# Fourth edge stage of a four-layer graph network: two of every 56 tiles gathered by SyncE and ScalarE

## The chip, the core and the metric

The kernel runs on one core of one Trainium2 chip. The core has a matrix engine (TensorE, PE in the profile), a vector engine (VectorE, DVE), an activation engine (ScalarE, ACT), a general engine (GpSimd, POOL) and a sequencer without arithmetic that issues DMAs (SyncE, SP), all of which run side by side and wait for each other on semaphores. Sixteen DMA engines move data between HBM and the on-chip memory. The metric is the device time of one execution in microseconds (us), the median of several.

## What is computed

Four graph layers run one after the other on 6250 nodes of 128 channels and the same 206250 edges, which are sorted by their target `dst`. Each layer normalises the nodes, gathers a row for each edge's source, and sums the rows per target. The fourth, the only one that the change touches, is the plainest:

```
def _L3_gnn_ref(x, edge_index, W, bias, ln_gamma, ln_beta):
    h = x @ W
    ...                      # src, dst: the edges and one loop per node
    deg = segment_sum(ones, dst)
    dinv = where(deg > 0, rsqrt(deg), 0)
    norm = dinv[src] * dinv[dst]
    agg = segment_sum(h[src] * norm[:, None], dst) + bias
    y = relu(layernorm(agg) * ln_gamma + ln_beta)
    return y + x
```

## The kernel before

The edges are cut into tiles of P = 128, four tiles (U = 4) to a group; 403 groups (EDGE_GROUPS), so 1612 tiles, hold all of them. Before the fourth edge stage the kernel has written `table3` to HBM: one row of 128 floats (512 bytes) per node, `h` times `dinv` of the source. The edge stage then does, for each tile, three things. GpSimd gathers the 128 rows of the tile's sources from `table3` with one indirect DMA (L1623), which takes the 128 node numbers from a column of `index`. VectorE makes, for a whole group at once, the matrices `hot` of zeros and ones (L189, in `one_hots`) that say which edge belongs to which of 128 consecutive targets. TensorE multiplies the rows by `hot` (L1681; every float32 product is two passes of the array, so 3224 matrix instructions) into `psS`, and VectorE adds the result to the window of `ACC` that begins at the tile's first target (L1656). The window's address comes from a register that VectorE's sequencer loads (L196, in `windows`).

The program of this stage is written out group by group, not as a loop, and the order on each engine is the order of the code. Four row buffers (R = 4) hold the rows of four groups. GpSimd may gather into a buffer when VectorE has done all additions of the group four before and has counted `s_done` up (L1620, L1658). TensorE waits for `hot` of its group, for the four tiles of rows, and for a free quarter of `psS`. VectorE makes `hot` one group ahead and then adds tile by tile. At the stage's start VectorE clears `ACC` (L1644) before it gives GpSimd its first four counts (L1645). SyncE loads `index` and three rows of parameters (L1610, L1612), and has nothing more to do until the stage is over; ScalarE scales 98 node tiles (L1632, L1636) and then has nothing more to do either. Once the last addition is done, a barrier of all engines (L1607) leads into the closing node stage.

Three other places are read below because they show what SyncE's and ScalarE's DMA instructions take. In the first edge stage SyncE issues, for each batch of 32 tiles, 32 DMAs whose source row is in a register (L632, 128 partitions each), after one register load for every four of them (L196), and between batches DMAs at fixed addresses (L641, L642), while ScalarE issues 512 KB loads (L679). In the second edge stage it issues windows (L1085, 128 partitions) and lengths (L1094, 8 partitions), both with the source row in a register. The program's first stage has loads at fixed addresses.

## Time and profile before

| | |
|---|---|
| median of 3 runs | 9777.23 us (9772.35 to 9777.35) |
| profiled execution, its own time | 9774.57 us |
| its span, first to last instruction | 9772.8 us |
| fourth edge stage, first gather to last addition | 7691.6 to 9709.3 us |
| share of the span: GpSimd, VectorE, TensorE, ScalarE | 74%, 65%, 54%, 18% |

The profile is of one execution. PE is TensorE's matrix work, PEld its weight loads, DVE VectorE, ACT ScalarE, POOL GpSimd, SP SyncE; a q behind an engine marks its sequencer. Lines are those of the kernel before. "issue" is time in which an engine waited for nothing that the profile shows. The shares over the whole span mix stages with different limits, so the change has to be read in the last fifth of the span, where its stage lies.

### The profile page before, as it was taken

The numbers are of one execution on the slowest core, as the hardware profiler recorded it, in microseconds if no ns is written. First come the engines' busy times: TensorE is split into PE (matmuls) and PEld (weight loads), VectorE is DVE, ScalarE is ACT, GpSimd is POOL, SyncE is SP. The second block draws the span as 40 slices with busy tenths as digits, with TensorE's granted clock in tenths as the row PEclk, the third lists the DMA queues.
The fourth block names the chain that finished last, engine by engine and source line by source line (L and its number), as shares of the span: only waits on it lengthen the run. The fifth ranks groups of instructions, "written<-read, shape, count | busy, mean of one in ns | idle before, by whom it ended". The sixth has DMA issues, their size and how long they took to land. (4 is left out here: it accounts for less than half of the span.)

```text
span 9772.8 us, 131915 instructions
## 1 busy us (share of the span) xinstructions
PE 5246.3 (54%) x29478; PEld 4593.4 (47%) x29478; DVE 6386.1 (65%) x17574; ACT 1742.3 (18%) x3229; POOL 7215.7 (74%) x6460
## 2 busy tenths in 40 slices
PE   2334333345555555555555488888888544444443
PEld 1333333334445444555555377777777433333333
DVE  4667766676777776666666588888888533333334
ACT  2222222221222222111111111111111200000001
POOL 3777777771888888888888477777777577777775
PEclk5555555556555555555555699999999655555555
DMA  5555554442776667777777422222222222222221
GB/s 137 130 121 125 125 129 112 117 116 63 111 111 109 109 110 112 113 109 108 109 110 112 101 56 56 56 57 57 57 56 56 54 53 53 53 53 53 53 53 52
DMA packets 1095241, 861.72 MB, mean 88 GB/s; under 512 B 408856, under 2 KB 931359, under 8 KB 1094342
## 3 DMA queue, kind: packets, MB, share of 16 engines
q0 software_dynamic: 386880, 427.12, 25.5%
q1 hardware_dynamic: 677460, 320.18, 14.4%
q10 hardware_dynamic: 30436, 109.19, 3.4%
q8 instruction: 174, 2.85, 0.1%
q14 instruction: 291, 2.38, 0.1%
HBM read 706.10 MB, written 149.64 MB: 88 GB/s over the span
## 5 line engine op out<-in xcount | busy, mean ns | idle before, releaser
L1286 POOL DMA_INDIRECT sums<-sumrows,index x1612 | 2521.8, 1564 | 674.5 <-issue 312.9
L670 POOL DMA_INDIRECT rows<-table,index x1612 | 1612.5, 1000 | 629.3 <-issue 485.6
L1623 POOL DMA_INDIRECT rows<-table,index x1612 | 1522.0, 944 | 570.5 <-issue 490.6
L1427 POOL DMA_INDIRECT rows<-table,index x1612 | 1547.7, 960 | 513.1 <-issue 393.7
L1681 PE MATMUL psS<-hot,rows 128*128 128x128 f32 x3224 | 824.7, 437 | 1207.4 <-issue 1142.4
L1681 PEld LDWEIGHTS psS<-hot,rows 128*128 128x128 f32 x3224 | 717.7, 328 | 1314.4 <-issue 1266.6
L1254 PE MATMUL psX<-same,hotW 128*128 128x128 f32 x3224 | 811.9, 431 | 970.3 <-DVE hotW L1157 970.0
L1656 DVE TENSOR_TENSOR ACC<-ACC,psS 128x128 f32 x1612 | 465.3, 289 | 1201.4 <-PE psS L1681 1087.9
L1254 PEld LDWEIGHTS psX<-same,hotW 128*128 128x128 f32 x3224 | 702.0, 320 | 1095.7 <-DVE hotW L1157 1095.1
L1263 PE MATMUL psV<-win,mix 128*128 128x129 f32 x3224 | 800.9, 425 | 346.4 <-ACT mix L1220 341.3
L1518 PEld LDWEIGHTS psS<-hot,mid 128*128 128x128 f32 x6448 | 869.9, 196 | 38.9 <-issue 5.7
L1263 PEld LDWEIGHTS psV<-win,mix 128*128 128x128 f32 x3224 | 686.7, 314 | 397.5 <-issue 397.5
L1518 PE MATMUL psS<-hot,mid 128*128 128x128 f32 x6448 | 868.8, 279 | 5.4 <-DVE mid L1484 4.0
L1454 DVE TENSOR_TENSOR ACC<-ACC,psS 128x256 f32 x1612 | 660.1, 410 | 17.3 <-PE psS L1518 12.7
L820 DVE TENSOR_TENSOR ACC<-ACC,psA 128x128 f32 x1612 | 465.5, 289 | 273.1 <-issue 65.8
L1174 DVE CAST index<-place 128x4 int32<-128x4 f32 x403 | 76.4, 189 | 782.1 <-DMA sums<-sumrows,index 781.7
L1503 PE MATMUL psA<-base,w 16*128 16x256 f32 x806 | 271.3, 416 | 368.5 <-issue 355.5
L1157 DVE TENSOR_SCALAR hotW<-K,REL,weight 128x128 f32<-128x128 f32 x1612 | 462.1, 371 | 0.0
L1224 ACT COPY sumrows<-psV 128x516 f32<-128x516 f32 x403 | 237.4, 589 | 1097.7 <-PE psV L1263 619.1
L1220 ACT COPY mix<-psX 128x512 f32<-128x512 f32 x403 | 236.2, 586 | 1101.6 <-PE psD L1257 1012.2
L1511 PE MATMUL psW<-w,h 128*128 128x128 f32 x3224 | 430.9, 277 | 1.1 <-ACT h L1439 1.1
L1437 ACT ACTIVATE h<-psA,b 128x256 f32<-128x256 f32 x403 | 191.1, 474 | 1169.8 <-PE psA L1503 1169.8
(303 smaller groups left out, 9559.0 us busy)
## 6 DMA issues: line engine op xcount, KB each, us to landing
win<-table SPq DMA_DIRECT2D x1612, 64.5 KB
srow<-src_f SPq DMA_DIRECT2D x403, 256.0 KB, 4.2
rows<-table,index POOLq DMA_INDIRECT x4836, 2.5
HN<-rel_f ACTq DMA_DIRECT2D x102, 512.0 KB, 4.4
relB<-rel_f ACTq DMA_DIRECT2D x102, 512.0 KB, 4.3
er<-limbs SPq DMA_DIRECT2D x1632, 3.0 KB
sums<-sumrows,index POOLq DMA_INDIRECT x1612
ACC<-edge_marks SPq DMA_DIRECT2D x204, 96.0 KB
```

The lines of the kernel that those rows point to most:

```text
L670: nc.gpsimd.indirect_dma_start(out=rows[:, r, k, :], out_offset=None, in_=table0[:, :], in_offset=bass.IndirectOffsetOnAxis(ap=index[:, n ...
L820: nc.vector.tensor_tensor(own, own, psA[:, j % 4, u * P:(u + 1) * P], ALU.add).then_inc(s_free, 1)
L1157: last = nc.vector.tensor_scalar(hotW[:, s, u, :], lane, REL[:, bass.ds(n * U + u, 1)], weight[:, bass.ds(n * U + u, 1)], ALU.is_equal, AL ...
L1254: last = nc.tensor.matmul(psX[:, u, :], hotW[:, s, u, :], same[:, s, u, :], start=True, stop=True)
L1263: last = nc.tensor.matmul(psV[:, s, u, 0:W1], mix[:, s, u, :], win[:, r, u, :], start=True, stop=True)
L1286: nc.gpsimd.indirect_dma_start(out=sums1[u][:, :], in_=sums[:, s, u, :], in_offset=None, compute_op=ALU.add, out_offset=bass.IndirectOffse ...
L1427: nc.gpsimd.indirect_dma_start(out=rows[:, n % R, u, :], out_offset=None, in_=table2[:, :], in_offset=bass.IndirectOffsetOnAxis(ap=index[: ...
L1454: nc.vector.tensor_tensor(own, own, psS[:, u, :, 0:P], ALU.add).then_inc(s_free, 1)
L1518: done = nc.tensor.matmul(psS[:, u, b, 0:P], mid[:, r % 2, u, b * C:(b + 1) * C], hot[:, r % 2, u, :], start=True, stop=True)
L1623: nc.gpsimd.indirect_dma_start(out=rows[:, n % R, u, :], out_offset=None, in_=table3[:, :], in_offset=bass.IndirectOffsetOnAxis(ap=index[: ...
L1656: nc.vector.tensor_tensor(own, own, psS[:, u, 0:P], ALU.add).then_inc(s_free, 1)
L1681: nc.tensor.matmul(psS[:, u, 0:P], rows[:, r, u, :], hot[:, r % 2, u, :], start=True, stop=True).then_inc(s_sum, 1)
```

## The change

SyncE and ScalarE each take one tile of every 14 groups off GpSimd. In groups 6, 20, 34, ... (29 of them) it is SyncE that gathers the fourth tile, in groups 13, 27, 41, ... (28 of them) ScalarE; GpSimd gathers only three tiles in these groups. A tile taken over is gathered row by row: the helper loads its 128 node numbers from HBM as one row of integers, loads them four at a time into registers, and issues one DMA of one row (512 bytes, into one partition) for each. So a tile costs its helper 32 register loads and 128 DMAs. The rows go into two buffers of the helper's own, used in turn; the node numbers are fetched one tile ahead.

The number of row buffers goes from 4 to 8 and of `hot` buffers from 2 to 3, and `psS` holds four whole groups instead of four tiles. GpSimd waits for TensorE's products of the group eight before (`s_sum`) instead of VectorE's additions of the group four before, and no longer waits for the clearing of `ACC`. VectorE makes `hot` of group n and then adds the results of group n - 2, and it waits for all four products of that group before the first of its additions. TensorE waits in a helper's group for the helper's 128 rows ahead of the fourth product.

```diff
-        gathered2, gathered3 = pool_sems("gathered2_", 4), pool_sems("gathered3_", 4)
+        gathered2, gathered3 = pool_sems("gathered2_", 4), pool_sems("gathered3_", 8)
...
-                R = 4
...
+                R = 8
+                RS = 3
                 index = sb("index3", [P, T], I32)
                 rows = sb("rows3", [P, R, U, C])
-                hot = sb("hot3", [P, 2, U, P])
-                psS = ps("psS3", [P, 4, 512])
+                hot = sb("hot3", [P, RS, U, P])
+                EVERY = 14
+                firsts_of = (("sp", 6), ("act", 13))
+                extra = {key: sb("rows3" + key, [P, 2, C]) for key, _ in firsts_of}
+                numbered = {key: sb("index3" + key, [1, 2, P], I32) for key, _ in firsts_of}
+                s_number = {key: sem("s_number_e3" + key, 2) for key, _ in firsts_of}
+                s_extra = {key: sem("s_extra_e3" + key, 2) for key, _ in firsts_of}
+                def helper(n):
+                    for key, at in firsts_of:
+                        if n % EVERY == at:
+                            return key
+                    return None
+                def tiles_of(n):
+                    return U if helper(n) is None else U - 1
+                def gathered_by(n):
+                    return sum(tiles_of(m) for m in range(n % R, n + 1, R))
...
+                def own_gather(eng, key, at):
...
+                    groups = list(range(at, EDGE_GROUPS, EVERY))
+                    def numbers_of(j):
+                        eng.dma_start(numbered[key][:, j % 2, :], a["src_rows"][groups[j] * U + U - 1:groups[j] * U + U, :]).then_inc(s_number[key][j % 2], 16)
+                    numbers_of(0)
+                    for j, n in enumerate(groups):
+                        if j + 1 < len(groups):
+                            numbers_of(j + 1)
+                        if j > 1:
+                            eng.wait_ge(s_sum, (groups[j - 2] + 1) * U)
+                        eng.wait_ge(s_number[key][j % 2], 16 * (j // 2) + 16)
+                        for p in range(0, P, U):
+                            _, sources = nc.values_load_multi_w_load_instructions(
+                                numbered[key][0:1, j % 2, p:p + U], engines=(eng.engine,), min_val=0, max_val=N - 1,
+                                skip_runtime_bounds_check_because="a src is a node number")
+                            for k in range(U):
+                                eng.dma_start(extra[key][p + k:p + k + 1, j % 2, :], table3[bass.ds(sources[k], 1), :]).then_inc(s_extra[key][j % 2], 16)
+                    for r in range(2):
+                        eng.wait_ge(s_extra[key][r], 16 * P * uses(len(groups), 2, r))
...
+                        own_gather(sp, *firsts_of[0])
...
                         for n in range(EDGE_GROUPS):
-                            pool.wait_ge(s_done, n + 1)
+                            if n >= R:
+                                pool.wait_ge(s_sum, (n - R + 1) * U)
                             pool.nop(nofuse=True)
-                            for u in range(U):
+                            for u in range(tiles_of(n)):
...
+                        own_gather(act, *firsts_of[1])
...
-                        dve.sem_inc(s_done, R)
-                        dve.sem_inc(s_free, 4)
-                        one_hots(hot[:, 0, :, :], 0, numbers).then_inc(s_hot, 1)
-
-                        def add(n, g, r):
-                            if not (isinstance(n, int) and n == last):
-                                one_hots(hot[:, (r + 1) % 2, :, :], n + 1, numbers).then_inc(s_hot, 1)
+                        def adds(n):
                             firsts = windows(dve, n * U)
                             for u in range(U):
-                                dve.wait_ge(s_sum, n * U + (u + 1))
-                                own = ACC[:, 0, bass.ds(firsts[u], P)]
-                                nc.vector.tensor_tensor(own, own, psS[:, u, 0:P], ALU.add).then_inc(s_free, 1)
-                                dve.wait_ge(s_free, n * U + (u + 5))
-                            dve.sem_inc(s_done, 1)
-
-                        dve.wait_ge(s_rowsB, 48)
-                        for g in range(TN // TG):
-                            for r in range(R):
-                                add(R * g + r, g, r)
-                                at = slice(g * TG, (g + 1) * TG)
-                                if r == 1:
-                                    dve.wait_ge(s_own, g + 1)
-                                    nc.vector.tensor_tensor(own[:, at, :], own[:, at, :], rowsB[:, 0, :].unsqueeze(1).to_broadcast([P, TG, C]), ALU.add)
-                                if r == 3:
-                                    dve.wait_ge(s_gate, g + 1)
-                                    nc.vector.tensor_tensor(X[:, at, :], X[:, at, :], hn[:, at, :], ALU.add)
-                        for n in range(R * (TN // TG), EDGE_GROUPS):
-                            add(n, n // R, n % R)
+                                dve.wait_ge(s_sum, (n + 1) * U)
+                                if n * U + u > 0:
+                                    dve.wait_ge(s_free, n * U + u)
+                                total = ACC[:, 0, bass.ds(firsts[u], P)]
+                                nc.vector.tensor_tensor(total, total, psS[:, n % 4, u, :], ALU.add).then_inc(s_free, 1)
+                        for n in range(EDGE_GROUPS):
+                            one_hots(hot[:, n % RS, :, :], n, numbers).then_inc(s_hot, 1)
+                            if n > 1:
+                                adds(n - 2)
...
+                        adds(EDGE_GROUPS - 2)
+                        adds(EDGE_GROUPS - 1)
...
-                        def sums(n, g, r):
+                        for n in range(EDGE_GROUPS):
                             pe.wait_ge(s_hot, n + 1)
-                            pe.wait_ge(s_rows[r], 16 * U * g + 16 * U)
+                            pe.wait_ge(s_rows[n % R], 16 * gathered_by(n))
+                            if n >= 4:
+                                pe.wait_ge(s_free, (n - 3) * U)
                             for u in range(U):
-                                pe.wait_ge(s_free, n * U + (u + 1))
-                                nc.tensor.matmul(psS[:, u, 0:P], rows[:, r, u, :], hot[:, r % 2, u, :], start=True, stop=True).then_inc(s_sum, 1)
-
-                        straight(EDGE_GROUPS, R, sums)
+                                own = rows[:, n % R, u, :]
+                                if u >= tiles_of(n):
+                                    key, j = helper(n), n // EVERY
+                                    pe.wait_ge(s_extra[key][j % 2], 16 * P * (j // 2 + 1))
+                                    own = extra[key][:, j % 2, :]
+                                nc.tensor.matmul(psS[:, n % 4, u, :], own, hot[:, n % RS, u, :], start=True, stop=True).then_inc(s_sum, 1)
```

GpSimd, in the fourth edge stage (rows: a tile's gather is one row, merged with its count).

```order
 L140 UNCONDITIONAL_BRANCH
-L1615 UNCONDITIONAL_BRANCH
-L1623 DMA rows<-table,index 128x128 x1612
-L1607 UNCONDITIONAL_BRANCH
+L1658 UNCONDITIONAL_BRANCH
+L1667 DMA rows<-table,index 128x128 x1555
+L1649 UNCONDITIONAL_BRANCH
```

GpSimd has 57 gathers fewer; its order is otherwise the same.

SyncE, at the start of the same stage: `index3sp` holds node numbers, `rows3sp` is SyncE's own buffer of rows, ISA is the register arithmetic ahead of a DMA.

```order
+L1654 DMA rowsB<-in_L_gnn_ln_beta 128x128
+L1624 DMA index3sp<-in_src_rows 1x128 x2
+L1634 TENSOR_LOAD index3sp [waits s_index_e03]
+L1638 ISA
+L1638 DMA rows3sp<-table 1x128
+L1638 ISA
+L1638 DMA rows3sp<-table 1x128
+L1638 ISA
+L1638 DMA rows3sp<-table 1x128
+L1638 ISA
+L1638 DMA rows3sp<-table 1x128
+L1634 TENSOR_LOAD index3sp
```

Where SyncE had nothing behind its fourth load, the pattern of one register load and four row DMAs stands 32 times for each of 29 tiles. ScalarE gets the same behind its 98 activations, for 28 tiles.

VectorE, the first additions of the stage, before:

```order
L1644 MEMSET ACC 128x6400
L189 TENSOR_TENSOR hot<-psK,REL 128x512 x2
L196 TENSOR_LOAD D
L1656 ISA
L1656 TENSOR_TENSOR ACC<-ACC,psS 128x128
L1656 ISA
```

and with the change:

```order
L1689 MEMSET ACC 128x6400
L189 TENSOR_TENSOR hot<-psK,REL 128x512 x2
L1710 TENSOR_TENSOR own<-own,rowsB 128x896
L189 TENSOR_TENSOR hot<-psK,REL 128x512
L196 TENSOR_LOAD D
L1698 ISA
L1698 TENSOR_TENSOR ACC<-ACC,psS 128x128
L1698 ISA
```

A third `hot` now stands ahead of the first addition, and the additions of a group stand one group further back; the number of instructions is the same.

## Rows read from the trace of the kernel before

**Rows 1.** Busy time by stretch: length, PE, PEld, DVE, ACT, POOL, TensorE clock, DMA share, GB/s.

```profile
1000.00:1400.00 400.00, 151.07 (x1012) 137.52 (x1012) 276.19 (x722) 90.76 (x94) 306.64 (x306) 0.59 0.54 127
8000.00:9000.00 1000.00, 409.47 (x1601) 356.18 (x1600) 370.17 (x1003) 0.00 (x0) 755.94 (x802) 0.50 0.20 53
```

**Rows 2.** Timeline in mid-stage: start, length, engine, line, operation, [idle before <-releaser].

```profile
8501.17 0.94 POOL L1623 DMA_INDIRECT rows<-table,index  x1 [0.30 <-issue]
...
8502.49 2.04 PE L1681 MATMUL psS<-hot,rows 128*128 128x128 f32 x8 [2.88 <-issue]
8503.39 0.29 DVE L1656 TENSOR_TENSOR ACC<-ACC,psS 128x128 f32 x1 [2.45 <-PE psS L1681]
...
8503.88 1.14 DVE L1656 TENSOR_TENSOR ACC<-ACC,psS 128x128 f32 x3 [0.21 <-PE psS L1681]
...
8505.17 0.69 DVE L189 TENSOR_TENSOR hot<-psK,REL 128x512 f32<-128x512 f32 x1
```

**Rows 3.** GpSimd's gathers of the fourth stage: ns min/median/max, first and last start.

```profile
L1623 POOL DMA_INDIRECT rows<-table,index x1612: 940/944/1187, 7691.6 to 9703.5; - x180
```

**Rows 4.** Waits from 7700 to 9700 us: total us, times, longest us.

```profile
POOL rows L1623 <- issue: 488.1, 1602, 0.3
```

**Rows 5.** GpSimd's gathers from 490 to 2200 us: busy us, mean ns, idle before.

```profile
L670 POOL DMA_INDIRECT rows<-table,index x1310 | 1312.4, 1002 | 399.3 <-issue 394.1 <-PE psA L851 5.2
```

**Rows 6.** Timeline at the fourth stage's start, one row of each engine.

```profile
7685.07 0.43 SPq L1612 DMA_DIRECT2D rowsB<-in_L_gnn_ln_beta  x1
...
7685.40 5.39 DVE L1644 MEMSET ACC<- 128x6400 f32 x1 [1.32 <-issue]
...
7691.62 0.94 POOL L1623 DMA_INDIRECT rows<-table,index  x1 [79.62 <-DVEq L1645]
...
7698.08 14.40 ACT L1636 ACTIVATE HN<-HN,RSTD 128x128 f32<-128x128 f32 x49
```

**Rows 7.** DMA issues of the page: count, KB each, median us to landing.

```profile
index<-in_src_cols SPq DMA_DIRECT2D x2, 816.0 KB, 4.5
...
index<-in_src_batches SPq DMA_DIRECT2D x51, 16.0 KB, 2.3
```

**Rows 8.** Timeline at the fourth stage's end.

```profile
9703.54 0.94 POOL L1623 DMA_INDIRECT rows<-table,index  x1 [0.30 <-issue]
...
9706.71 2.04 PE L1681 MATMUL psS<-hot,rows 128*128 128x128 f32 x8 [3.56 <-issue]
...
9708.11 1.14 DVE L1656 TENSOR_TENSOR ACC<-ACC,psS 128x128 f32 x3 [0.21 <-PE psS L1681]
```

**Rows 9.** Sequencers' DMA and register-load instructions by line: ns min/median/max, starts.

```profile
L632 SPq DMA_DIRECT2D er<-limbs x1632: 332/333/24072, 97.2 to 2159.7; - x182
...
L1094 SPq DMA_DIRECT2D radius<-in_weight_rows x808: 276/277/349, 2410.5 to 5395.0; - x162
...
L641 SPq DMA_DIRECT2D ACC<-edge_marks x204: 302/421/1583, 151.5 to 2176.6; - x102
...
L642 SPq DMA_DIRECT2D rowm<-tile_marks x51: 298/310/336, 153.4 to 2177.1; - x51
...
L429 ACTq DMA_DIRECT2D ends_i<-in_dst_last x1: 328/328/328, 6.0 to 6.0; - x1
...
L196 DVEq TENSOR_LOAD <-D x1209: 337/343/604, 196.0 to 9703.8; - x173
L196 SPq TENSOR_LOAD <-D x811: 293/301/1444, 95.5 to 5401.8; - x163
```

**Rows 10.** Timeline of SyncE's issues: start, us from first start to last end, count.

```profile
1011.24 19.47 SPq L632 DMA_DIRECT2D er<-limbs  x32
...
1012.82 1.17 SPq L632 DMA_DIRECT2D er<-limbs  x2
...
1014.18 0.85 SPq L632 DMA_DIRECT2D er<-limbs  x2
...
3001.09 2.15 SPq L1094 DMA_DIRECT2D radius<-in_weight_rows  x5
```

More of the change, by code:

```diff
@@ L1594, in build @@
                 sb, ps, sem = alloc(st)
-                R = 4
-                last = EDGE_GROUPS - 1
+                R = 8
+                RS = 3
                 index = sb("index3", [P, T], I32)
                 rows = sb("rows3", [P, R, U, C])
-                hot = sb("hot3", [P, 2, U, P])
-                psS = ps("psS3", [P, 4, 512])
+                hot = sb("hot3", [P, RS, U, P])
+                EVERY = 14
+                firsts_of = (("sp", 6), ("act", 13))
+                extra = {key: sb("rows3" + key, [P, 2, C]) for key, _ in firsts_of}
@@ L1601, in build @@
+                psS = ps("psS3", [P, 4, U, P])
                 numbers = ps("psK3", [P, 512])[:, 0:P]
-                s_chain, s_hot, s_sum, s_free, s_done = (sem(n + "_e3") for n in ("s_chain", "s_hot", "s_sum", "s_free", "s_done"))
+                s_chain, s_hot, s_sum, s_free = (sem(n + "_e3") for n in ("s_chain", "s_hot", "s_sum", "s_free"))
                 s_rows = gathered3
@@ L1626, in _ @@
                         for r in range(R):
-                            pool.wait_ge(s_rows[r], 16 * U * uses(EDGE_GROUPS, R, r))
+                            pool.wait_ge(s_rows[r], 16 * gathered_by(EDGE_GROUPS - 1 - (EDGE_GROUPS - 1 - r) % R))
                     @block.scalar
@@ new lines, in _ @@
+                        for n in range(EDGE_GROUPS):
+                            one_hots(hot[:, n % RS, :, :], n, numbers).then_inc(s_hot, 1)
+                            if n > 1:
+                                adds(n - 2)
+                            g, r = divmod(n, 4)
+                            at = slice(g * TG, (g + 1) * TG)
+                            if n == 0:
+                                dve.wait_ge(s_rowsB, 48)
+                            if g < TN // TG and r == 1:
+                                dve.wait_ge(s_own, g + 1)
+                                nc.vector.tensor_tensor(own[:, at, :], own[:, at, :], rowsB[:, 0, :].unsqueeze(1).to_broadcast([P, TG, C]), ALU.add)
+                            if g < TN // TG and r == 3:
+                                dve.wait_ge(s_gate, g + 1)
+                                nc.vector.tensor_tensor(X[:, at, :], X[:, at, :], hn[:, at, :], ALU.add)
```

## The prediction, made before the changed kernel had run

> **What bounds the kernel now.** I read the busy time by stretch first, because the shares of the whole span mix the stages. From 8000 to 9000 us, the inside of the fourth edge stage, GpSimd is busy 756 of 1000 us and no other engine over 410; ScalarE does nothing and the DMA engines are 20% busy [rows 1]. The timeline shows the pattern: gathers of 0.94 us, each after 0.30 us of idle time that waits for nothing [rows 2], 1602 such gaps, 488 us, and practically no wait for another engine [rows 4]. So GpSimd issues without a pause, and a tile costs (9703.5 - 7691.6) / 1611 = 1.249 us [rows 3]. A group's four tiles take 5.0 us. VectorE works on a group for 0.69 us of `hot` and four additions, each (1.14 - 0.29) / 2 = 0.43 us after the one before, 2.4 us together, and waits for TensorE's products; TensorE works for 2.04 us and idles 2.9 [rows 2]. TensorE's granted clock is 0.50, the 1.2 GHz level, all through [rows 1], and nothing in this sum needs the other. The stage's time is the number of GpSimd's gathers times 1.249 us, and a start and an end.
>
> **What GpSimd sheds.** SyncE takes 29 tiles and ScalarE 28, so 57 of 1612 gathers go: 57 x 1.249 = 71.2 us, all on the path, if the helpers keep up. At the start GpSimd no longer waits for the clearing of `ACC`, which ends at 7690.8, 0.8 us ahead of the first gather [rows 6]. What is late next is the index: issued some 1.3 us ahead of the last row of parameters, so at 7683.7 to 7684.1, and 4.5 us to landing [rows 6, 7], 7688.6. With the same 0.8 us the first gather starts at 7689.4, 2.2 us earlier. At the end VectorE now waits for all four products of the last group. Before, its last addition ended at 9709.25, 5.7 us after the last gather began; now it has four additions, 4 x 0.43, behind the last product, about 1.9 us after TensorE's start at 9706.7: 9710.3, so 1.0 us more [rows 8]. Net: 71.2 + 2.2 - 1.0 = 72.4 us, and the stage would end at 9636.9.
>
> **What it costs elsewhere if the helpers keep up.** VectorE has the same instructions in another order, under a cover of 5.0 - 2.4 = 2.6 us a group. TensorE has the same products. The two new waits on TensorE (helper's rows, additions four groups back) have queued behind them all later products, and so VectorE and, eight groups on, GpSimd. That is the question to price: when is a helper's tile there?
>
> **What a helper's tile costs.** No row shows SyncE copying one row into one partition from a register address, so I bound it. The nearest rows with the source in a register: 0.333 us for 128 partitions (L632), 0.277 for 8 (L1094). With a fixed address: 0.421 us for 32 partitions (L641), 0.310 for one (L642) [rows 9]. So the instruction gets shorter as the copy narrows, and a register address doesn't lengthen it. The ends are 0.333 - (0.421 - 0.310) = 0.222 us and 0.310 us. I take 0.23, near the lower end: the register row for 8 partitions is at 0.277 already, and one partition must lie under it by the trend of both pairs. Around each DMA stand the register instructions: two starts are 0.85 - 0.333 = 0.517 us apart, 0.184 us besides the DMA; five of L1094 give (2.15 - 0.277) / 4 - 0.277 = 0.191, as much [rows 10]. A register load between two DMAs adds 1.17 - 0.333 - 0.517 = 0.32 us [rows 10]. Then there is a remainder: 32 DMAs with 7 loads should take 31 x 0.517 + 7 x 0.32 + 0.333 = 18.6 us and took 19.47 [rows 10], in a stage with 54% DMA share [rows 1]. Per tile of 128 that is 0 to 3.5 us; in the quiet fourth stage I take 1.1, and 0.4 for the load of the node numbers (0.310 [rows 9] and a gap). SyncE's tile: 128 x (0.23 + 0.184) + 32 x 0.32 + 1.5 = 53.0 + 10.2 + 1.5 = **64.7 us**. ScalarE's one fixed-address row copy is 0.018 us longer than SyncE's (0.328 against 0.310) and its register load is not shown; between SyncE's 0.301 and VectorE's 0.343 [rows 9]. That makes 64.7 to 64.7 + 2.3 + 1.3 = 68.3 us; I take 66.5.
>
> **How long it may take.** Fourteen groups have 54 gathers left on GpSimd, 54 x 1.249 = 67.4 us. SyncE starts at about 7688 (its first node numbers are issued behind the parameters at 7685.5 and take about 2.3 us to land [rows 6, 7]). Its first tile has landed and been multiplied at 7688 + 64.7 + 2.3 + 1 = 7756.0; GpSimd needs the buffer of group 6 for group 14, after 54 gathers, at 7689.4 + 67.4 = 7756.8. That just fits, and then SyncE gains 2.7 us each round. The eight buffers are what pays for SyncE's late first tile: TensorE stands at group 6 for some 30 us, then VectorE clears eight groups at 2.4 us each while GpSimd makes one in 5. ScalarE starts after its activations, 7698.1 + 14.4 = 7712.5 [rows 6], so at 7715 with its numbers; its first tile is through at 7715 + 66.5 + 3.3 = 7784.8, and GpSimd needs it for group 21, after 81 gathers, at 7790.6. At the end, SyncE's 29th tile (group 398) sets the end when 7688 + 29 t + 3 and the additions of five groups (about 11 us), 7702 + 29 t, come after 9636.9: from t = 66.7 us. ScalarE's 28th (group 391, twelve groups at 2.4 us behind it) gives 7747 + 28 t: from t = 67.5. The old end, 9709.3, is reached at 69.2 and at 70.1 us.
>
> A rule speaks against the change. The DMA engines are at 20%, and the tile's bound is the time of issue, 1.249 us for 64 KB [rows 1, 3]. The Trainium skill, page DMA: Bandwidth & Descriptors, section Issuing engines are not separate DMA queues, says that issuing from several engines saves only the sequencer's time, usually small beside the DMA itself. Here that time is the whole bound, so by the trace the rule's exception holds.
>
> **The rivals.** (1) The helpers are late by a little: SyncE's tile at 66.7 to 69.2 us or ScalarE's at 67.5 to 70.1. Each us over costs 29 or 28 us. At 68.0 for SyncE the end is 7702 + 1972 = 9674, gain 35, time 9742. For it: my limit is only 2.0 us, 0.016 us per row, above my estimate. Against: the estimate has the remainder in already.
>
> (2) SyncE becomes the bound and the kernel is slower. It decides from 69.2 us a tile, a DMA instruction of 0.265 us. At L1094's 0.277 the tile is 128 x 0.461 + 11.7 = 70.7 us, the end 7702 + 2050 = 9752, time 9777 + 43 = 9820; at 0.310 the tile is 74.9, the end 9874, time 9942. For it: no row has a register-addressed copy under 0.276. Against: both pairs fall with the width.
>
> (3) A fixed price for each DMA instruction, whatever its width, like L641's 0.421 us [rows 9] in place of 0.23: the tile is 128 x 0.605 + 11.7 = 89.1 us, the end 7702 + 2584 = 10286, time 10354. The rows at 0.277 and 0.333 speak against it. The Trainium skill has such a price: its page DMA: Bandwidth & Descriptors gives, in the comparison under Why a DMA increments its semaphore by 16 and not by 1, 512 cycles of the sequencer for the instruction on earlier generations, and Advanced Engine Details and Errata, Clock Domains, 1.2 GHz for that sequencer, by estimate 0.427 us; this case's trace shows less in two rows of three, so it does not bear the rule out.
>
> (4) The relief doesn't come through because the row DMAs slow GpSimd's own gathers. Where SyncE issued row loads and the DMA share was 54%, a gather took 1.002 us on the mean [rows 1, 5], 0.058 more: 1555 x 0.058 = 90 us, a loss of 18, time 9795. Against: VectorE was busy 69% of that stage (276 of 400 us) and 37% of this [rows 1], and the fourth stage's DMA share stays near 20%, since the bytes are the same.
>
> **How the numbers follow.** Full gain: 0.67. Rival 1: 0.16, two thirds of it faster by over 0.2%. Rival 2: 0.12. Rival 3: 0.01. Rival 4: 0.04, in part only. Against the profiled execution's own time the forecast is 9774.57 - 72.4 = 9702.2 us; the median lay 2.7 us above that execution, so 9705 us. Below it there is little: the 1.0 at the end, the start, and run to run spread, 9697. Above, full gain and rival 1 together hold 0.83, so the range must reach through rival 1: 9770. About 0.2% (20 us) is what a measurement of this kernel can tell from no change. Faster by over that: 0.67 + 0.11 + 0.01 of rival 4 = 0.79; within: 0.06; slower: 0.15.
>
> **What would show it.** Right: GpSimd 1555 gathers, still 1.249 us apart with "issue" before them; 128 rows of SyncE in 63 to 66 us; the stage's last addition 72 us after an earlier start by 2. Rival 1 or 2 shows as TensorE waiting for a DMA of `rows3sp` or `rows3act` to the end of the stage and as gaps of GpSimd released by TensorE; the DMA instruction's duration (0.23, 0.277 or 0.31) decides between them. Rival 4 shows as gathers of over 0.95 us. The forecast is wrong if a row copy takes over 0.246 us on SyncE, or if the remainder per tile is over 3.1 us.

## The result and the profile after

The changed kernel is slower: 9980.46 us (9971.51 to 9987.03, four runs) against 9777.29 us (9772.35 to 9780.23, four runs), a ratio of 1.0208 with a 95% interval of 1.0196 to 1.0221. That is 203 us more, where I had forecast 72 less. The profiled execution took 9977.01 us, its span is 9975.2 us. The kernels called e1 to e4 below ran on one chip, e13 and e14 on another, where every kernel took longer (the kernel before 11199 and 11188 us) and instructions of the sequencers stalled now and then (472 of the 3712 address moves of SyncE in e2 by some 0.67 us, none of them in e5); from these, e1's ratio apart, only medians of durations are read, and where a line is the same in both programs they agree (L196 on SyncE: 301 ns there too).

In the kernel after, GpSimd's gather is L1667, TensorE's product L1730, VectorE's addition L1698, a helper's register load L1634 and its row DMA L1638. First the helpers' instructions (ns min/median/max, first and last start), which answer to [rows 9]:

```profile
L1634 SPq TENSOR_LOAD <-index3sp x928: 463/557/767, 7689.5 to 9823.6; - x186
L1634 ACTq TENSOR_LOAD <-index3act x896: 478/587/802, 7711.3 to 9882.9; - x180
...
L1638 SPq DMA_DIRECT2D rows3sp<-table x3712: 224/225/312, 7690.2 to 9825.6; - x196
...
L1638 ACTq DMA_DIRECT2D rows3act<-table x3584: 224/224/540, 7711.9 to 9885.0; - x200
```

The row DMA takes the 0.23 us that I had put in. The register load takes 0.557 and 0.587 us, where the rows of before had 0.301. From its first to its last row DMA SyncE needs 9825.6 - 7690.2 = 2135.4 us for 29 tiles, 73.6 each; ScalarE 2173.1 us for 28, 77.6 each. Both are above the 67.4 us that GpSimd needs for the 54 gathers of 14 groups, and above the 69.2 and 70.1 at which the old end was to be reached.

The waits from 7690 to 9900 us (total us, times, longest us) answer to [rows 4]:

```profile
DVE ACC L1698 <- PE psS L1730: 1380.7, 568, 41.5
...
PE psS L1730 <- DMA rows3act<-table: 985.5, 28, 39.7
POOL rows L1667 <- issue: 409.6, 1340, 0.9
POOL rows L1667 <- PE psS L1730: 329.0, 208, 11.0
...
PE psS L1730 <- DMA rows3sp<-table: 197.7, 10, 36.1
```

TensorE stands for each of ScalarE's 28 tiles, 35 us each time, and for ten of SyncE's. GpSimd, which had waited for nobody, now waits 329 us for products that stand behind these waits. Its gathers themselves answer to [rows 3], the stretch from 8000 to 9000 us to the second of [rows 1], the additions to [rows 8]:

```profile
L1667 POOL DMA_INDIRECT rows<-table,index x1555: 939/947/1829, 7690.3 to 9906.5; - x195
...
8000.00:9000.00 1000.00, 291.90 (x1456) 259.28 (x1456) 307.64 (x914) 0.00 (x0) 661.31 (x700) 0.59 0.19 49
...
L1698 DVE TENSOR_TENSOR ACC<-ACC,psS x1612: 276/289/292, 7699.7 to 9913.2; 128x128 f32 x180
```

57 gathers are gone and the duration of those left has hardly moved (median 947 against 944 ns, mean 950 against 944), but they are 9906.5 - 7690.3 = 2216 us from first to last where 1554 x 1.249 would be 1941. In 1000 us GpSimd makes 700 instead of 802. The last addition ends at 9913.5 instead of 9709.25: 204 us, the whole loss, lies in this stage. TensorE's granted clock is 0.59 there, a mean of its two levels (1.2 GHz is 0.50, 2.4 GHz 1.00), and was 0.50: it idles for up to 40 us, then makes the products of three groups without a pause and those of the next ones with pauses of about 1 us, in which it waits for `hot`. Three stretches at the end of the stage (the last wait for ScalarE's rows, and the work behind it):

```profile
9846.00:9886.00 40.00, 1.62 (x6) 1.36 (x6) 0.86 (x2) 0.00 (x0) 24.52 (x26) 0.50 0.17 46
9886.00:9891.00 5.00, 4.62 (x26) 4.43 (x26) 2.65 (x9) 0.00 (x0) 2.60 (x3) 0.67 0.10 25
9891.00:9896.00 5.00, 2.32 (x16) 1.94 (x16) 3.80 (x12) 0.00 (x0) 3.78 (x5) 1.00 0.21 56
```

The clock is 0.50 while TensorE stands, and 1.00 from 9891 to 9896 us. The higher clock does not shorten the stage: the helpers' rows are what TensorE waits for.

### The profile page after: what moved, and what is told of

The parts are those of the page before. It is cut to its first block and busy times, and to the rows that moved or that the text cites. A ratio compares the mean times of both kernels' runs of the same rounds, so it can differ in the third digit from the quotient of the medians.

```text
span 9975.2 us, 155677 instructions
## 1 busy us (share of the span) xinstructions
PE 5068.7 (51%) x29478; PEld 4447.9 (45%) x29478; DVE 6315.6 (63%) x17574; ACT 1743.1 (17%) x3229; POOL 7167.8 (72%) x6403
## 5 line engine op out<-in xcount | busy, mean ns | idle before, releaser
L1286 POOL DMA_INDIRECT sums<-sumrows,index x1612 | 2521.9, 1564 | 672.2 <-issue 316.2
L670 POOL DMA_INDIRECT rows<-table,index x1612 | 1610.1, 999 | 633.8 <-issue 485.0
L1667 POOL DMA_INDIRECT rows<-table,index x1555 | 1476.8, 950 | 817.5 <-issue 411.4
L1427 POOL DMA_INDIRECT rows<-table,index x1612 | 1547.2, 960 | 515.5 <-issue 391.2
L1698 DVE TENSOR_TENSOR ACC<-ACC,psS 128x128 f32 x1612 | 462.2, 287 | 1529.2 <-PE psS L1730 1382.2
L1518 PEld LDWEIGHTS psS<-hot,mid 128*128 128x128 f32 x6448 | 867.7, 196 | 37.6 <-issue 4.7
L1730 PE MATMUL psS<-hot,rows 128*128 128x128 f32 x3110 | 627.6, 372 | 395.2 <-DVE hot L189 227.3
L1730 PEld LDWEIGHTS psS<-hot,rows 128*128 128x128 f32 x3110 | 560.3, 273 | 459.4 <-DVE hot L189 279.3
L1730 PE MATMUL psS<-hot,rows3act 128*128 128x128 f32 x56 | 22.3, 501 | 985.5 <-DMA rows3act<-table 985.5
L1730 PEld LDWEIGHTS psS<-hot,rows3act 128*128 128x128 f32 x56 | 14.0, 310 | 993.6 <-DMA rows3act<-table 993.6
```

Source lines behind the costliest of these rows:

```text
L670: nc.gpsimd.indirect_dma_start(out=rows[:, r, k, :], out_offset=None, in_=table0[:, :], in_offset=bass.IndirectOffsetOnAxis(ap=index[:, n ...
L1286: nc.gpsimd.indirect_dma_start(out=sums1[u][:, :], in_=sums[:, s, u, :], in_offset=None, compute_op=ALU.add, out_offset=bass.IndirectOffse ...
L1427: nc.gpsimd.indirect_dma_start(out=rows[:, n % R, u, :], out_offset=None, in_=table2[:, :], in_offset=bass.IndirectOffsetOnAxis(ap=index[: ...
L1518: done = nc.tensor.matmul(psS[:, u, b, 0:P], mid[:, r % 2, u, b * C:(b + 1) * C], hot[:, r % 2, u, :], start=True, stop=True)
L1667: nc.gpsimd.indirect_dma_start(out=rows[:, n % R, u, :], out_offset=None, in_=table3[:, :], in_offset=bass.IndirectOffsetOnAxis(ap=index[: ...
L1698: nc.vector.tensor_tensor(total, total, psS[:, n % 4, u, :], ALU.add).then_inc(s_free, 1)
```

## The experiments

Three theories are named in what was expected. **T**: the helpers' time per tile sets the end, as the prediction's formulas say, and buffers and order cost nothing. **K**: a register load takes 0.56 instead of 0.30 us because of the kind of DMA that its engine issued since the load before (one partition wide here, 128 in L632's stage). **M**: it takes longer because of what it reads (`index3sp`, freshly loaded, instead of `D`).

### Buffers and order alone

```diff
+                HELPED = ()
-                    for key, at in firsts_of:
+                    for key, at in HELPED:
...
-                        own_gather(sp, *firsts_of[0])
-                        own_gather(act, *firsts_of[1])
```

> The change without its helpers: eight row buffers, three of hot, additions two groups behind, but GpSimd gathers all 1612 tiles. Theory T (the helpers' tiles are late because a register load takes 0.56 to 0.60 us instead of 0.32, everything else costs nothing): the old time less the 2.2 us of the earlier start plus 1.0 us at the end, 9776 us, gathers 1.249 us apart. Rival R (the new order of VectorE's additions or the waits for whole groups cost time themselves, some 0.5 us a group): over 9850 us, with GpSimd released by TensorE or VectorE.

It (e1) took 11154.93 us against 11199.46, 0.9966 (0.9952 to 0.9981). The same kernel again, on another chip (e8):

> The kernel of e1 once more, beside a kernel before at its usual time: no helpers, eight row buffers, additions two groups behind. Theory T: 9776 us, ratio 0.9999. Rival R: above 1.002.

It took 9760.26 us, ratio 0.9998 (0.9988 to 1.0007). GpSimd's gathers (first and last start) span what they did:

```profile
L1667 POOL DMA_INDIRECT rows<-table,index x1612: 940/944/1841, 7671.6 to 9683.9; - x180
```

2012.3 us for 1611, 1.249 each. Eight buffers, `psS` for four groups and additions two groups behind neither cost nor save. The loss belongs to the helpers.

### One helper alone

```diff
-                    for key, at in firsts_of:
+                    for key, at in firsts_of[:1]:
...
-                        own_gather(act, *firsts_of[1])
```

> The change with SyncE as the only helper; ScalarE's 28 tiles go back to GpSimd, which then has 1583. Theory T: SyncE's tiles take 73.5 us as they did beside ScalarE, so 7702 + 29 x 73.5 = 9833 us is the stage's end and the time about 9777 + 125 = 9902 us, 78 us under the change, because ScalarE's 28 tiles of 77.6 us (end 7747 + 2173 = 9920) were what the change waited for. Rival C (the two helpers slow each other on the one DMA engine or queue that they share): SyncE's tile falls well under 73.5, towards 65 us, and the time towards 9750.

It (e6, two runs) took 9879.92 us, 1.0121 (1.0101 to 1.0141), 117 us more than before; 125 more were expected. SyncE's load and TensorE's wait:

```profile
L1634 SPq TENSOR_LOAD <-index3sp x928: 458/558/733, 7678.7 to 9807.8; - x186
...
PE psS L1729 <- DMA rows3sp<-table: 1018.4, 29, 38.0
```

So the two helpers don't disturb each other: SyncE's load and its tile (73.5 us) are the same without ScalarE. It alone makes the kernel slower, and TensorE now stands for all 29 of its tiles; with both, ScalarE's slower tile hides most of that.

### Fewer loads, of more numbers

One load of 16 numbers in place of four of four (and of 8 in a second kernel, whose edit has 8 where this one has 16); the DMAs stay.

```diff
-                        for p in range(0, P, U):
+                        for p in range(0, P, 16):
...
-                                numbered[key][0:1, j % 2, p:p + U], ...
+                                numbered[key][0:1, j % 2, p:p + 16], ...
-                            for k in range(U):
+                            for k in range(16):
```

> The change with 16 node numbers per register load instead of 4, so 8 loads a tile instead of 32; nothing else. Theory T: SyncE's tile falls by 24 x (0.57 + 0.03 + 0.035) = 15 us from 73.5 to about 58, ScalarE's by 24 x (0.60 + 0.03 + 0.24) = 21 us from 77.6 to about 57, both under the 67.4 us that GpSimd needs for its 54 gathers, so GpSimd sets the end and the time is 9705 us. If the time of a load grows with its registers (0.56 us being 0.14 each), the tiles stay at 73 and 77 us and the time at 9980. Rival C (the row DMAs themselves hold the sequencers up, through one busy DMA engine): the DMA instructions get longer as they come faster, tiles over 67 us.

It (e2) took 12350.71 us on the chip of e1 (1.1038, 1.1016 to 1.1059), where SyncE's tile took 120.6 us on the mean, the stalls with it. That ratio is not the edit's, as the same kernel shows on another chip (e5):

> The kernel of e2 once more, 16 node numbers per register load, beside a kernel before that is at its usual 9777 us. From the loads and row DMAs of e2's undisturbed stretches (load 1.23 us on SyncE and 1.29 on ScalarE, row DMA 0.225): SyncE's tile is 128 x 0.408 + 8 x 1.28 + 1.4 = 64 us, ScalarE's 128 x 0.38 + 8 x 1.55 + 1.4 = 63 us, both under 67.4. Theory T: GpSimd sets the end again, time 9705 us, ratio 0.9926. Rival C (a helper's row DMAs hold something else up): GpSimd's gathers above 0.96 us or further apart than 1.249, time above 9740.

It took 9690.08 us (9685.65 to 9695.99), ratio 0.9925 (0.9908 to 0.9942): this version beats both kernels. (The 58 us a tile of e2's expectation had a load at 0.57 us whatever its size; it takes 1.230.) Its loads, its gathers, and GpSimd's idle time by releaser (us, times):

```profile
L1634 SPq TENSOR_LOAD <-index3sp x232: 1133/1230/1415, 7677.6 to 9530.7; - x116
L1634 ACTq TENSOR_LOAD <-index3act x224: 1193/1299/1464, 7699.6 to 9495.5; - x112
...
L1667 POOL DMA_INDIRECT rows<-table,index x1555: 940/945/1739, 7678.4 to 9625.2; - x195
...
  issue: 414.4, 1358
...
  PE psS L1730: 59.8, 196
```

From one tile's first row DMA to the next one's SyncE needs 64.0 us in the median, ScalarE 62.7, both below 67.4, and the gathers run 1946.8 us for 1554, 1.253 each. The gain is 9762.45 - 9690.08 = 72.4 us. The prediction had 72.4 for helpers that keep up, but that the two agree to the decimal is luck: by the interval of the ratio the gain is 57 to 90 us, and in the profiled execution the gathers span 65.1 us less than in the kernel before (2011.9), not 71.2.

> The change with 8 node numbers per register load (16 loads a tile), between the change and the 16 of e5. Loads of 4 numbers took 0.56 us and of 16 1.23, so 8 should take 0.56 + 4 x 0.056 = 0.78 on SyncE and 0.82 on ScalarE. SyncE's tile: 128 x 0.408 + 16 x 0.845 + 1.4 = 67.1 us, ScalarE's 128 x 0.38 + 16 x 1.08 + 1.4 = 67.3: level with the 67.4 of GpSimd's period. Theory T: SyncE's end 7702 + 29 x 67.1 = 9648, 11 us over GpSimd's, time 9716 us, ratio 0.994.

With loads of 8 (e12; median 792 and 825 ns) it took 9712.05 us, 0.9950 (0.9934 to 0.9967). Both tiles take 67.4 us, just the budget; by the prediction's formula, shifted to the first row's start (7676.4 instead of 7688), SyncE's end would be 7690.4 + 29 x 67.4 = 9645, and VectorE's last addition starts at 9642.8.

### What makes the load long

In all of these kernels but the last (e9) the helpers' tiles no longer hold the sources' rows; the number of loads and of row DMAs and the waits are those of the changed kernel.

> The change with the helpers' register loads reading the table of first targets (the tile that the register loads of the first edge stage read) instead of the helper's own node numbers, 4 numbers each as before; the rows of the helpers' 57 tiles are therefore not the reference's. Theory M (what is read decides): loads at 0.30 us, SyncE's tile 73.5 - 32 x 0.26 = 65.2 us. Theory K (the DMAs ahead of the load decide): loads stay at 0.56 us on SyncE and 0.59 on ScalarE, time about 9980 us.

```diff
-                                numbered[key][0:1, j % 2, p:p + U], ...
+                                D0[0:1, p:p + U], ...
```

```profile
L1634 SPq TENSOR_LOAD <-D x928: 3/555/1460, 8775.2 to 12496.6; - x186
L1634 ACTq TENSOR_LOAD <-D x896: 3/586/1396, 8828.4 to 12357.6; - x180
```

Reading the memory that L196 reads, with 0.301 us, the load still takes 0.555. M falls. (This was e4, on the chip of e1, with 12574.54 us.)

> The change with each of a helper's 128 DMAs writing 16 partitions of 32 bytes instead of one partition of 512; the data of the helpers' 57 tiles is therefore not the reference's, the bytes and the number of instructions are. Theory K (a register load is slow behind a DMA of few partitions, because of something that such a DMA leaves to the sequencer): the load falls to 0.30 us as in the first edge stage, the DMA instruction rises to about 0.32, tile 128 x 0.50 + 32 x 0.33 = 75 us on SyncE. Theory M (the load is slow for what it reads, the helper's buffer of node numbers): the load stays at 0.56 us and the tile is 128 x 0.50 + 32 x 0.6 = 83 us.

```diff
-   eng.dma_start(extra[key][p + k:p + k + 1, j % 2, :], table3[bass.ds(sources[k], 1), :])
+   eng.dma_start(extra[key][(p + k) % 8 * 16:(p + k) % 8 * 16 + 16, j % 2,
+                 (p + k) // 8 * 8:(p + k) // 8 * 8 + 8], table3[bass.ds(sources[k], 16), 0:8])
```

```profile
L1634 SPq TENSOR_LOAD <-index3sp x928: 2/298/1402, 8780.8 to 12534.8; - x186
L1634 ACTq TENSOR_LOAD <-index3act x896: 3/308/1385, 8832.9 to 12306.7; - x180
...
L1638 SPq DMA_DIRECT2D rows3sp<-table x3712: 2/316/1574, 8781.5 to 12536.7; - x196
```

The same number of DMAs and loads, each DMA 16 partitions wide: the load falls to 0.298 us, L196's own value, and the DMA rises to 0.316, near L632's. The chip isn't the cause: e4, on the same one, had 0.555. From one load to the next it is 2.320 us in the median; less four DMAs with their register work, 4 x (0.316 + 0.184) = 2.000, a load adds 0.32 us, just the prediction's price. It (e3) took 12612.86 us. The repeat (e14) came to another chip that stalls, with 12617.86 us and the same two medians:

> All row DMAs write 16 partitions of 32 bytes (the gathered rows of the helpers' tiles are not the sources' rows, everything else is computed as in the changed kernel). Alternation theory (a load costs 0.26 us more behind DMAs that are narrower than 16 partitions): load 0.30 and 0.31 us, DMA 0.32 and 0.33, no dearer first DMA behind a load, so SyncE's tile 32 x 0.30 + 128 x (0.32 + 0.20) = 76.2 us, ScalarE's 32 x 0.31 + 128 x (0.33 + 0.20) = 77.8 us, and a time of about 7702 + 29 x 76.2 = 9912 against 7747 + 28 x 77.8 = 9925 for the stage's end, so about 9990 us. If the 0.30 of the first run belonged to the disturbed chip, the load is 0.56 and 0.59 here and the tiles are 84.5 and 86.8 us, the time 10240.

```profile
L1634 SPq TENSOR_LOAD <-index3sp x928: 3/298/1394, 8776.6 to 12539.8; - x186
L1634 ACTq TENSOR_LOAD <-index3act x896: 4/308/1387, 8829.9 to 12305.1; - x180
```

So neither of its two forecast times could be tried; the durations repeat. What of a row of DMAs counts was asked by three more kernels, of the same form as the last diff: 8 partitions of 64 bytes; three rows and then one DMA of 16 partitions; three of 16 partitions and then one row (e10, e11, e13).

> The change with each of a helper's DMAs writing 8 partitions of 64 bytes, between the change (one partition) and e3 (sixteen); the data of the helpers' tiles is not the reference's. Theory K1 (any DMA of fewer than 16 pieces makes the next load slow): load at 0.47 to 0.56 us on SyncE, DMA instruction 0.277 as in the second edge stage, tile 128 x 0.46 + 32 x 0.58 = 77 us. Theory K2 (the load gets slow in proportion to what is missing to sixteen): load about 0.42 us.

> The change with only the last of each four DMAs, the one just ahead of the next register load, writing 16 partitions of 32 bytes; the other three write one partition as in the change. The data of the helpers' tiles is not the reference's. Theory K with the last DMA deciding: load at 0.30 us. Theory K with any narrow DMA since the last load deciding: load stays at 0.56.

> Of each four DMAs the first three write 16 partitions (32 bytes each), the last one partition (512 bytes); the gathered rows of the helpers' tiles are therefore not the sources' rows, everything else is computed as in the changed kernel. Last-DMA theory: a register load waits for what the DMA just ahead of it left behind, so with a narrow one ahead it takes 0.56 us on SyncE and 0.59 on ScalarE, as in the changed kernel. Mixture theory: every narrow DMA since the load before counts, and three wide ones shorten it, so the load lies between 0.30 and 0.49, below what one wide and three narrow ones gave. Tile of SyncE by the first: 73.6 + 96 x 0.095 = 82.7 us, time about 10240 us; by the second 0.1 to 0.26 us a load less, 74.5 to 79.5 us a tile, 10000 to 10150.

Their loads in this order:

```profile
L1634 SPq TENSOR_LOAD <-index3sp x928: 460/558/794, 7678.5 to 10023.4; - x186
```

```profile
L1634 SPq TENSOR_LOAD <-index3sp x928: 457/492/652, 7684.9 to 9851.2; - x186
```

```profile
L1634 SPq TENSOR_LOAD <-index3sp x928: 3/536/1393, 8765.8 to 12652.5; - x186
```

Behind DMAs of 8 partitions the load is as dear as behind one (and the DMA takes 0.277 us, L1094's value; the kernel 10189.62 us). SyncE's tile took 80.9 us and not the 77 expected: that sum had neither the gap behind a load nor the first DMA behind it, 0.312. One narrow DMA among three wide ones, ahead of the load, gives 0.536; one wide one ahead of the load and three narrow ones before it, 0.492 (10007.47 us); on ScalarE it is 0.505 and 0.492. So the DMA just ahead matters a little and doesn't decide. Of the two theories of the last kernel, the first said 0.56 and the second under 0.49; neither holds in full, the first is nearer; its times could not be tried on a chip that stalls. Only where all DMAs since the last load are 16 or 128 partitions wide is the load at 0.30. The size of the pieces changes with the width in e3 and e10, but other rows set it aside: 8 partitions of 1024 bytes each (L1094, below) go with a dear load as 8 of 64 bytes do, and 128 of 24 (L632) or 2048 bytes (L1082) with a cheap one.

> The change with the register loads of 16 rows standing together: four loads of 4 numbers, then 16 row DMAs; as many loads and DMAs as in the change. Theory K (a load is slow because of the narrow DMA just ahead of it): the first load of each four takes 0.56 us and the other three 0.30, SyncE's tile falls from 73.5 by 24 x 0.26 and by 24 x 0.035 (the long DMA behind a load comes once in 16) to 66.4 us, ScalarE's from 77.6 by 24 x 0.28 and 24 x 0.23 to 65.4. Theory A (a load of this kind takes 0.56 us wherever it stands): all four at 0.56, tiles at 73 and over 71 us.

```diff
-                        for p in range(0, P, U):
+                        for p in range(0, P, 4 * U):
+                            four = []
+                            for c in range(4):
...                                    # one load of four numbers, added to four
-                            for k in range(U):
-                                eng.dma_start(... sources[k] ...)
+                            for k in range(4 * U):
+                                eng.dma_start(... four[k] ...)
```

This is the plainest of all: the same 928 loads of four numbers and the same 3712 row DMAs, only four loads in a row and then 16 DMAs. All loads, then (e9, one run) from one batch the first alone, then that first and its three followers:

```profile
L1636 SPq TENSOR_LOAD <-index3sp x928: 292/296/785, 7681.9 to 9605.2; - x186
...
L1636 SPq TENSOR_LOAD <-index3sp x1: 551/551/551, 7848.7 to 7848.7; - x1
...
L1636 SPq TENSOR_LOAD <-index3sp x4: 293/294/551, 7848.7 to 7849.9; - x4
```

The load behind a DMA takes 0.551 us, the three behind a load 0.293 to 0.296. SyncE's tile is 66.5 us, ScalarE's 64.8, both within 0.6 us of what was expected, and the kernel took 9700.05 us in its one run where the one of before took 9761.05 (9751.73 to 9770.74, seven runs). What the changed kernel pays is not for the load, but for each turn from narrow DMAs to a load and back.

### A longer round

> The change with a helper's tile every 17 groups instead of every 14 (24 tiles for SyncE and 23 for ScalarE), nothing else. GpSimd then needs 66 x 1.249 = 82.4 us a period, over both helpers' 73.5 and 77.6. Theory T: GpSimd sets the end, 47 x 1.249 = 58.7 us and 1.2 us of start and end saved, time 9717 us, ratio 0.9939. Rival R (eight buffers and additions two groups behind cost time, or the helpers' late tiles cost GpSimd its pace): time at 9777 or above.

```diff
-                EVERY = 14
+                EVERY = 17
```

It (e7) took 9718.94 us, 0.9955 (0.9939 to 0.9972), a little less gain than the 0.9939 expected. The helpers have 66 gathers, 82.4 us, for a tile of 74 or 78, and the 1565 gathers should be 1564 x 1.249 = 1953 us from first to last:

```profile
L1667 POOL DMA_INDIRECT rows<-table,index x1565: 939/945/1484, 7676.6 to 9645.2; - x196
...
7711.97 1.62 PE L1730 MATMUL psS<-hot,rows 128*128 128x128 f32 x6 [1.15 <-issue]
7751.20 0.80 PE L1730 MATMUL psS<-hot,rows3sp 128*128 128x128 f32 x2 [37.62 <-DMA rows3sp<-table]
```

They are 1969, and the difference lies at the start (busy GpSimd of a stretch; its wait for TensorE in it):

```profile
7676.00:7800.00 124.00, 88.48 (x89) 0.57 0.19 49
```

```profile
POOL rows L1667 <- PE psS L1730: 11.0, 10, 8.3
```

There are 89 gathers in 124 us, where 99 would fit. TensorE is done with group 6's first three products at 7713.6 and stands 37.6 us for SyncE's first tile; group 14's buffer, for which GpSimd comes after 54 gathers at 7676.6 + 67.4 = 7744, is free only behind 7751.2, the 8.3 us. Some of the gathers are longer (0.994 us on the mean) and make up most of the rest. SyncE's first tile takes 73.5 us, and its product comes 8.0 us after GpSimd is due: the eight buffers cover a first tile of 65.5 us, however rare the later ones are.

## Why the prediction was wrong

**What held.** The bound and the price of a gather (1.249 us) stand: the kernel whose helpers keep up gains 72 us (57 to 90; loads of 16), where my sum had 72.4. The first gather began 4.2 us behind the start of the clearing of `ACC`, where it had been 6.2: 2.0 of the 2.2 us.

```profile
7686.08 5.39 DVE L1689 MEMSET ACC<- 128x6400 f32 x1 [1.32 <-issue]
...
7690.28 0.95 POOL L1667 DMA_INDIRECT rows<-table,index  x1 [77.08 <-DMA index<-in_src_cols]
```

The row DMA, the term that I had held for the most uncertain, came out at 0.225 of 0.23, with 0.183 us of register work beside it of 0.184. What came in is the outcome of rival 2, a SyncE tile above 69.2 us and a slower kernel, to which I had given 0.12; its cause, a dearer DMA instruction, did not, and nor did rival 3's. The price of 0.427 us that the prediction cites from the Trainium skill, page DMA: Bandwidth & Descriptors, section Why a DMA increments its semaphore by 16 and not by 1, is borne out by no row DMA but ScalarE's first behind each load, 0.457. Rival 4 failed: gathers 950 ns on the mean, not 1002. The end formulas held: with 77.6 us ScalarE's gives 7747 + 28 x 77.6 = 9920, and the last addition ended at 9913.5.

**The step that failed** is "A register load between two DMAs adds 1.17 - 0.333 - 0.517 = 0.32 us" [rows 10]. It had one value and no second bound, though its row came from between DMAs of 128 partitions, and 32 such loads stand in a tile. In the changed kernel four DMAs with their load take SyncE 2.248 us in the median and ScalarE 2.378, by start times of the loads. Without the load, SyncE's four would take 4 x (0.225 + 0.184) = 1.636, ScalarE's, whose starts are 0.381 apart, 1.524. So a load adds **0.61 us** on SyncE and **0.85** on ScalarE. Three parts make it up: the load itself, 0.557 and 0.587 instead of 0.30; the gap behind it; and the first DMA behind it, which is longer than the others, here one of each engine alone:

```profile
L1638 SPq DMA_DIRECT2D rows3sp<-table x1: 260/260/260, 7782.4 to 7782.4; - x1
...
L1638 ACTq DMA_DIRECT2D rows3act<-table x1: 457/457/457, 7811.5 to 7811.5; - x1
```

Put in, the sum closes: SyncE 32 x 2.248 = 71.9 and a remainder of 1.7 (I had 1.5) is 73.6 against my 64.7; ScalarE 32 x 2.378 = 76.1 and 1.5 is 77.6 against my 66.5, of which 32 x 0.23 = 7.5 us is the first DMA alone. SyncE's 8.9 us too many, 29 times, are 258 us, ScalarE's 11.1, 28 times, 311; and my estimates lay only 2.0 and 1.0 us under the first loss. The stage ends with ScalarE: (11.1 - 1.0) x 28 = 283 us late by the formula, and the time is 275 us above my 9705.

**What I could have seen.** The trace of before has the dear load too. In the second edge stage, L1094's DMAs of 8 partitions come in every fourth group, and between them and the next load stands one DMA of 128 (L1082). SyncE's loads from 2990 to 3100 us, then the one at 3004.8, which stands behind such DMAs:

```profile
L196 SPq TENSOR_LOAD <-D x14: 296/300/472, 3004.8 to 3098.1; - x14
...
L196 SPq TENSOR_LOAD <-D x1: 470/470/470, 3004.8 to 3004.8; - x1
```

The very batch of [rows 10] from which I took my price begins with one, behind the one-partition DMA of L642; I took the price from the loads after it:

```profile
L196 SPq TENSOR_LOAD <-D x8: 295/304/462, 1010.6 to 1028.4; - x8
```

Sorted by whether a DMA of L642 or L1094 stands between a load and the load before it, all 811 loads of SyncE in that trace fall into two kinds: the 151 with one take 0.462 to 0.503 us, and of the 660 without, 657 take 0.293 to 0.367. So the rule that the experiments found lay in the trace of before.

The 0.47 beside a median of 0.30 was the second bound: 32 x 0.17 = 5.4 us a tile more, 70.1 for SyncE, past the 69.2 at which the kernel gets slower. The Trainium skill, page DMA: Bandwidth & Descriptors, section Latency and other measured facts, gives a register load a floor of about 600 ns. The rows of before do not bear that out as a floor (medians of 0.301 on SyncE, 0.343 on VectorE), nor does e9 (0.296); the changed kernel's 0.557 and 0.587 come near the figure. I had left it out, and with it a rival: by an estimate from that page 32 x 0.3 = 9.6 us a tile more, 74.3 in all. The 73.6 measured lie near it, though the load's own time gives only 32 x 0.26 = 8.3 us of them; the gap and the first DMA behind it are the rest.

Also wrong was the discriminator. I wrote that the DMA instruction's duration decides between the outcomes, and that the forecast falls if a row copy takes over 0.246 us or the remainder is over 3.1. Neither happened (with the load at its measured price the remainder is 1.7) and it fell, since the list of what could fail had the terms that I doubted and not the one that I had copied. ScalarE's own load, of which I said that no row shows it, got 0.04 us of margin; it needed 0.53.

**What stays open.** Why a load behind narrow DMAs takes longer. The runs show that it is the width of the DMAs since the last load (1 or 8 partitions dear, 16 or 128 not; nothing between 8 and 16 was tried), not what is read, and not the number of helpers. That the sequencer waits there for something that narrow DMAs leave behind fits all of them, and is argued, not shown; nor is it shown why ScalarE's first row DMA costs 0.457 us and SyncE's 0.260.

## What to carry to other kernels

Price a repeated pattern as a whole, from a place where the same neighbours stand side by side: a load from between wide DMAs says nothing of one between narrow ones. A term multiplied by 32 and then by 29 needs two bounds even if its row looks firm; the maximum beside the median in a row is one to be had for nothing, and what stood ahead of the dear ones is worth a look. Where rows are copied one by one from addresses in registers, load many addresses in a row, or many with one load, before the DMAs (loads of 16 numbers turned 2.1% slower into 0.75% faster here).

## What the runs showed of the hardware

- A register load of four numbers on SyncE took 0.296 us behind another load, 0.298 behind DMAs of 16 partitions, 0.557 behind DMAs of 1 or 8, 0.46 to 0.54 behind narrow and wide ones mixed; loads of 8 and 16 numbers took 0.792 and 1.230, so some 0.056 us for each number more.
- A register-addressed DMA instruction on SyncE took 0.225 us for one partition, 0.277 for 8, 0.316 for 16, 0.333 for 128.
- The first narrow DMA behind a load, or behind wide ones, took 0.26 us on SyncE and 0.46 on ScalarE. In the kernel with three wide DMAs and then a narrow one it is the last of the four:

```profile
L1643 SPq DMA_DIRECT2D rows3sp<-table x928: 3/264/1408, 8768.6 to 12654.7; - x186
L1643 ACTq DMA_DIRECT2D rows3act<-table x896: 3/467/718, 8823.4 to 12492.6; - x180
```

- 7296 row DMAs of 512 bytes beside them left GpSimd's gathers at medians of 944 to 947 ns.
